# Cache copies on one queue in 4 or 8 parts, value and weight splits on GpSimd, one scale on ScalarE, in a two-layer attention kernel

## The reference, cut to what matters

```python
x = x + einsum('bsi,boi->bso', x, weight[adapter_ids])        # layer 0, 8 batches of 128x512
# layer 1: attention, 32 query heads, 8 key heads, D = 128
q, k, v = x@Wq.T, x@Wk.T, x@Wv.T                               # q: 8 x 4 x 128 columns, k and v: 8 x 128
q = rope(rmsnorm(q, q_norm_w)); k = rope(rmsnorm(k, k_norm_w))
kc, vc = k_cache[block_table], v_cache[block_table]            # 16 pages of 32 rows for each batch
scores = einsum(q, concat(kc, k)) / sqrt(D)                    # 512 cached keys and 128 new ones
probs = softmax(where(valid, scores, -1e30))
x = x + (probs @ concat(vc, v)) @ Wo.T
```

## Time and profile before

| what | value |
|---|---|
| median of 2 runs | 1092.32 us (1089.48 and 1095.16) |
| the profiled execution's own time | 1094.0 us |
| its span in the profile | 1092.0 us |
| PE busy | 977.4 us, 90% of the span |
| DVE busy | 920.3 us, 84% |
| POOL busy | 863.5 us, 79% |
| ACT busy | 796.4 us, 73% |
| mean granted TensorE clock | 0.97 of full speed |
| moved by DMA | 173.69 MB, mean 159 GB/s |

### The profile page before, as it was taken

The page is one execution under the profiler, slowest core; times in us unless marked ns, Lnnn a source line. Parts: engine busy times, 40 slices in busy tenths (PEclk is TensorE's granted clock), DMA queues, the critical chain, the costliest instruction groups (busy, mean ns, idle before and its releaser), DMA issues.

```text
span 1092.0 us, 20813 instructions
## 1 busy us (share of the span) xinstructions
PE 977.4 (90%) x5617; PEld 559.3 (51%) x5617; DVE 920.3 (84%) x1942; ACT 796.4 (73%) x2202; POOL 863.5 (79%) x1184
## 2 busy tenths in 40 slices
PE   6787997789868999989998999899998999899997
PEld 4344554455434555545554555455555555455554
DVE  6576876578868999989997999979997999899994
ACT  4364655468677888878887888878887888777873
POOL 3656567558858998889898998889888988989881
PEclk9889999899999999999999999999999999999999
DMA  8688977738897777766778677876776777757862
GB/s 256 174 230 239 246 229 221 207 106 160 179 187 137 142 154 157 138 136 142 158 140 162 128 144 157 148 145 140 154 139 139 153 158 140 130 99 133 152 140 64
DMA packets 505733, 173.69 MB, mean 159 GB/s; under 512 B 429121, under 2 KB 487762, under 8 KB 505618
## 3 DMA queue, kind: packets, MB, share of 16 engines
q1 hardware_dynamic: 482752, 149.76, 65.5%
q10 hardware_dynamic: 21714, 20.25, 6.1%
q0 software_dynamic: 1152, 2.36, 0.8%
HBM read 98.11 MB, written 31.86 MB: 119 GB/s over the span
## 4 chain that ended last, share of the span: by engine, by line
PE 42%; DVE 19%; issue 4%; POOL 2%; ACT 2%; DVEq 0%; POOLq 0%; ACTq 0%
PE S L1729 10%; DVE pr L1359 5%; DVE pr L1331 5%; DVE sm L1344 4%; PE Y L1655 4%; PE Y L1657 4%; PE Y L1656 4%; PE Q L1656 3%; PE Q L1655 3%; PE Q L1657 3%; PE O L1655 2%; PE O L1656 2%; PE O L1657 2%; PE T L1661 2%; POOL wl L644 2%
## 5 line engine op out<-in xcount | busy, mean ns | idle before, releaser
L1359 DVE SCALAR_TENSOR_TENSOR pr<-pr,rc,upper 128x640 f16<-128x640 f32 x220 | 235.2, 1069 | 20.5 <-ACT upper L1025 13.8
L1331 DVE CUSTOM_DVE_ANT_0 pr<-S,mask,rst 128x640 f32<-128x640 f32 x256 | 224.4, 876 | 30.8 <-PE S L1729 19.2
L1025 ACT ACTIVATE upper<-pr,rc 128x640 f16<-128x640 f32 x220 | 170.3, 820 | 75.7 <-DVE rc L1347 75.6
L1045 ACT ACTIVATE pr<-pr,nb 128x640 f32<-128x640 f32 x256 | 209.6, 819 | 17.5 <-DVE nb L1331 14.5
L1729 PE MATMUL S<-kh,qh 128*128 128x320 f16 x512 | 113.0, 303 | 41.9 <-DVE nb L1331 41.9
L754 POOL TENSOR_TENSOR m<-m 128x512 f32<-128x512 f32 x63 | 81.7, 1297 | 78.1 <-DVE m L1403 78.1
L1729 PE MATMUL S<-kl,qh 128*128 128x320 f16 x512 | 112.3, 301 | 0.9 <-POOL kl L644 0.9
L1729 PE MATMUL S<-kh,ql 128*128 128x320 f16 x512 | 112.5, 302 | 0.0
L644 POOL TENSOR_TENSOR wl<-wraw,wh 128x512 f16<-128x512 f32 x71 | 104.2, 1468 | 5.9
L1729 PEld LDWEIGHTS S<-kh,qh 128*128 128x128 f16 x512 | 45.9, 99 | 116.1 <-DVE nb L1331 71.1
L1655 PE MATMUL Q<-wh,xh 128*128 128x512 f16 x256 | 99.9, 390 | 4.1 <-issue 2.8
(11 more groups left out here) (218 smaller groups left out, 2719.4 us busy)
## 6 DMA issues: line engine op xcount, KB each, us to landing
wraw<-in_wall SPq DMA_DIRECT2D x74, 256.0 KB, 3.5
cache_rows<-in_kv ACTq DMA_DIRECT2D x80, 224.0 KB
rawk<-cache_rows SPq DMA_DIRECT2D x55, 256.0 KB
vraw<-cache_rows SPq DMA_DIRECT2D x55, 256.0 KB, 4.6
cache_rows<-in_kv SPq DMA_DIRECT2D x36, 224.0 KB
second<-in_lw SPq DMA_DIRECT2D x4, 1024.0 KB
first<-in_lw SPq DMA_DIRECT2D x3, 1024.0 KB
cache_rows<-in_kv SPq DMA_DIRECT2D x16, 192.0 KB, 3.6
```

The lines of the kernel that those rows point to most:

```text
L1025: e.activation(upper16[:, g, :], pr[:, slot(u, g), :], ACT.Copy, scale=rc[:, u % 2, g:g + 1]).then_inc(a_f1, 1)
L1045: e.activation(pr[:, slot(u, g), :], pr[:, slot(u, g), :], ACT.Exp, bias=nb[:, u % 2, g:g + 1], scale=-1.0, accum_out=sm[:, u % 2, g:g + 1 ...
L1331: e.tensor_tensor_reduce(pr[:, slot(u, g), :].rearrange("p (a n) -> p a n", a=2), S[:, :, 0:320], mask[:, u % NB, :].rearrange("p (a n) -> ...
L1359: e.scalar_tensor_tensor(out=lower16(u, g), in0=pr[:, slot(u, g), :], scalar=rc[:, u % 2, g:g + 1], in1=upper16[:, g, :], op0=ALU.mult, op ...
```

## The change

Each piece in a sentence:

- NL goes from 9 to 4. Units 4 to 8 load keys and values from the copy.
- All copies are issued by SP, 16 pages (one batch) in each of periods 0 to 7, batches 4, 5, 6, 7, 0, 1, 2, 3. Batches 4 to 7 copy 16 rows a page in 4 parts (pieces of 4 KB), batches 0 to 3 copy 14 rows in 8 parts (2 KB).
- The tables: weight loads, squares and high parts come about one period earlier, the low parts stay about where they were. The two slots in a period are gone. DVE's three low parts of head 0 go to POOL.
- The value split of periods 1 to 8 goes from DVE (2 operations) to POOL (3).
- `score_scales` goes from POOL to ACT, between `q_hi` and `new_k_hi`. `norm` makes the variance in one operation rather than two. `kvr` is made in two operations rather than one (`value_back`).
- The first unit's key split goes to ACT and DVE; chunk 5 of head 0 has its high part on POOL.

```diff
-NL = NB + 1
+NL = 4
-COPY_SP = (0, 1, 1, 1, 1, 1, 1, 2, 0, 1, 1, 1, 2, 0)
-COPY_ACT = (2, 2, 3, 2, 2, 3, 3, 2, 1, 0, 0, 0, 0, 0)
-LO_DVE = {(0, 6): (1, 1), (0, 7): (1, 1), (0, 9): (1, 1)}
+LO_POOL = {(0, 6): 1, (0, 7): 1, (0, 8): 1, (0, 9): 1, (1, 0): -4, (1, 1): -4, (1, 2): -3,
+           (1, 3): -3, (1, 4): -2, (1, 5): -2, 0: -6, 1: -5, 2: -4, 3: -3, 4: -2, 5: -2,
+           6: -1, 7: 0, 8: 1, 9: 1}
+LOAD_AT = {(1, 0): -8, (1, 1): -8, (1, 2): -7, (1, 3): -7, (1, 4): -7, (1, 5): -6,
+           0: -12, 1: -11, 2: -11, 3: -10, 4: -9, 5: -8, 6: -6, 7: -6, 8: -5, 9: -5}
...
+def copies_of(period):
+    return [((period + NL) % NB, t) for t in range(NGRP)] if 0 <= period < NB else []
...
         def copy_page(e, b, k, number):
-            rows = slice(2 if b >= NL - NB else 4, 2 * NK)
-            e.dma_start(copy[rows, b, k, :].rearrange("r (s n) -> s r n", s=16),
-                        kv[rows, bass.ds(number, 1), :].rearrange("r a (s n) -> (a s) r n", s=16)
+            rows, parts = (slice(2, 2 * NK), 8) if b < NL else (slice(0, 2 * NK), 4)
+            e.dma_start(copy[rows, b, k, :].rearrange("r (s n) -> s r n", s=parts),
+                        kv[rows, bass.ds(number, 1), :].rearrange("r a (s n) -> (a s) r n", s=parts)
...
             def load_w(hk, c):
-                if hk >= 1:
+                if hk >= 1 and c < 4:
+                    e.wait_ge(w_lo[0], parts_made(hk - 2, 0) + c + 1)
+                elif hk >= 1:
                     e.wait_ge(w_lo[group(c)], parts_made(hk - 1, group(c)))
...
             for i in range(0, NA):
+                if i + 3 < NB:
+                    load_x(i + 3)
+                if NL <= i + 1:
+                    load_v(i + 1)
                 if 2 <= i + 1 < NB:
                     load_mask(i + 1)
                 next_weights(i)
                 if i + 3 < NL:
-                    for t in range(NT):
+                    for t in range(2, NT):
                         load_kt(e, kt_regs, i + 3, t)
-                        if t == (1 if i else 0) and i + 3 < NB:
-                            load_x(i + 3)
-                else:
-                    load_k(e, i + 3)
                 for b, t in copies_of(i):
                     copy_pages(b, t)
+                if i + 3 >= NL:
+                    load_k(e, i + 3)
...
+            def score_scales(j):
+                e.wait_ge(g_pow, j + 1)
+                e.wait_ge(g_kvr, j + 1)
+                if j >= 2:
+                    e.wait_ge(v_max, 4 * (j - 1))
+                e.activation(rst[:, j % 2, 0:G], pw[:, j % 2, 0:G], ACT.Copy,
+                             scale=f32(kvr[:, j % 2, 1:2])).then_inc(a_rst, 1)
```

More of the change, by code:

```diff
@@ L99, in at_period @@
         for c in range(NWC):
-            own = hk == 0 or (table is LO_POOL and (hk, c) in LO_DVE)
-            if not ((hk, c) in table or (c in table and not own)):
-                continue
-            at = table[(hk, c)] if (hk, c) in table else table[c]
-            if at == (period - NB * hk if slot is None else (period - NB * hk, slot)):
+            general = c in table and hk > 0 and not (hk == 1 and c < 6)
+            at = table.get((hk, c), table[c] if general else None)
+            if at is not None and NB * hk + at == period:
                 found.append((hk, c))
     return found
-def copies_of(period, act=False):
-    if not 0 <= period < len(COPY_SP):
-        return []
-    first = sum(COPY_SP[:period]) + sum(COPY_ACT[:period]) + (COPY_SP[period] if act else 0)
-    return [((k // NGRP + NL) % NB, k % NGRP)
-            for k in range(first, first + (COPY_ACT if act else COPY_SP)[period])]
+def copies_of(period):
+    return [((period + NL) % NB, t) for t in range(NGRP)] if 0 <= period < NB else []
 def build(nc, x, xt, lw, wall, kv, ids_lens, table, pages, qkw, consts, iota, out):
@@ L358, in build @@
         id_reg = nc.sync.alloc_register("id")
-        copy_regs = [nc.scalar.alloc_register(f"copied{j}") for j in range(12)]
+        copy_regs = [nc.scalar.alloc_register(f"copied{j}") for j in range(4)]
         def bc(src, n):
@@ L569, in _ @@
             e.dma_start(kwc[:, :], qkw[D:2 * D].unsqueeze(1)).then_inc(d_kwc, 16)
-            for t in range(2):
+            for t in range(3):
                 load_kt(e, kt_regs, 0, t)
@@ L649, in _, with split_w @@
             w_scaled = [0]
-            def split_w(period, place):
-                for hk, c in at_period(LO_POOL, period, place):
+            def split_w(period):
+                for hk, c in at_period(LO_POOL, period):
                     e.wait_ge(w_hi[group(c)], hi_made(hk, c))
@@ L866, in _ @@
                     gather_v(j, 1)
+                if i == 0:
+                    keys_hi(j)
+                    keys_lo(j)
+                q_sum(j)
+                norm(j)
                 if i:
                     keys_hi(j)
-                norm(j)
-                keys_lo(j)
-                split_w(i, 0)
-                split_w(i, 1)
+                    keys_lo(j)
+                split_w(i)
                 if 1 < j < NL:
@@ L1006, in v_squares, with first_keys_hi @@
                 square(v_left[:, u % 2, :], vraw[:, u % 3, :], kvss[:, u % 2, 0:1]).then_inc(a_kvss, 1)
[L1008 to L1017 removed]
+            def first_keys_hi():
+                e.wait_ge(g_kvs, 1)
+                e.activation(kh[:, 0, 0:512], raw_k(0), ACT.Copy, scale=k_scale(0)
+                             ).then_inc(made_kh, 1)
+            def score_scales(j):
[5 more added lines that the diff above has]
+                             scale=f32(kvr[:, j % 2, 1:2])).then_inc(a_rst, 1)
             def upper_plane(u, g):
@@ L1071, in _ @@
             split_chunk(0, 4)
-            split_chunk(0, 5)
+            w_square(0, 1)
             l0_hi(0)
-            for c in range(1, 4):
+            for c in range(2, 4):
                 w_square(0, c)
-            key_squares(0)
             for c in range(4):
                 split_chunk(0, c)
+            key_squares(0)
             k_squares(0)
@@ L1114, in _ @@
                     exp(i, 1)
+                    for t in range(2):
+                        load_kt(e, copy_regs, 3, t)
                 q_squares(j)
@@ L1512, in _ @@
             k_sum(0)
+            first_keys_lo()
             q_lo(0)
```

271 lines of the change are left out of this document (112 added, 159 removed), and 12 rows, old and new, of tables (HI_ACT, LO_POOL, SQUARES).

## The result

The changed kernel takes 1202.01 us (median of 2 runs, 1201.38 and 1202.63), against 1092.32 before. The ratio is 1.100, with a 95% interval of 1.088 to 1.113: slower, on the predicted side and inside the range, 19 us under the predicted 1221. The profiled execution took 1202.63 us; its span is 1200.8 us, its mean granted TensorE clock 0.923.

The account below looks back on a forecast made before the run. The kernel was taken as bound early by when transfers land, later by PE. 1094.0 + 151 (periods 0 to 8) - 13.7 (periods 9 to 13) - 10.8 (heads' starts) gave 1220.5, forecast 1221 us, range 1075 to 1285.

Parts of the forecast that it names:

- The deciding choice: Copies in periods 0 to 7: one engine per outermost index, so four or eight engines carry them; chance 0.78.
- Rival A: Periods 0 to 8: copies use all 16 engines, a batch takes 11 us, the whole 1066 us; chance 0.13.
- the heads' starts: Six new heads after period 14: POOL late by 0.95 us less, and 0.85 goes in period 25; -10.8 us.
- Rival B: Periods 0 to 8: copies on all 16 engines, but POOL becomes the early bound; 1090 us, chance 0.09.
- The first copy: Period 0: SP issues it at about 52 us, after x, weight chunks and eight 16 KB loads.
- The price of a piece: Copies: 177 ns per 4 KB and 94 ns per 2 KB piece; a batch takes 45.3 or 21.1 us.
- what lies around the copies: Periods 0 to 8: other loads add 7, 7 and 3 us to the first two batches, then 8 + 3.
- The weights that hold SP: Periods 4 and 5: chunk loads waiting for POOL's low parts delay the copies; keys come 15 us late each time.
- Periods 9 to 13: With all copies in by then, their 13.7 us over five plain periods go: -13.7 us.
- Period 25 and its like: Period 25, 0.87 us over a plain one: period 24's second POOL chunk moves to 25, so 0.85 us goes.
- the plain periods: From period 14 on, at 14.3 us each: PE stays full, so 0 change.
- The new wait of ACT's `rst`: Heads' starts: ACT's `rst` waits for POOL's power, ahead of new keys and last exponential; -3 to +10 us, 0 taken.

Follow-up runs that it names:

- e1: The changed kernel with every page's copy cut into 16 parts, nothing else touched; 1096.48 us, ratio 1.0005 to the kernel before.
- e4: The changed kernel with all copies cut in 8 parts, so batches 4 to 7 too; 1127.51 us.
- e3: The kernel before with its copies in 4 parts instead of 16 and one repeated group of pages left out; 1191.1 us.
- e9: e1 with SP's load of the next keys moved ahead of the copies of the same period; 1072.65 us.
- e5: The changed kernel with SP's weight loads of periods 0 to 7 moved behind the period's copies and keys' load; 1188.24 us.
- e12: The changed kernel with POOL's variance in two operations again and nothing else changed; 1186.48 us.
- e6: e1 with `score_scales` moved back from ACT to POOL, behind the keys' low part and ahead of the weight chunks; 1097.79 us.

## Why the prediction was right, and where it was off

**The deciding choice was right.** A copy runs on as many engines as it has parts: e1, e4 and e3 show it, each by its own way. Rival A was wrong in its condition, and e1, which meets the condition, shows its size too: 1096 and not 1066. The 16 engines finish early, but the load of the keys stands behind 16 copies that end inside the period, so the keys wait 54 us in seven periods, where the rival had 18 in two. e9 takes that away and comes to 1073. Its gain at the heads' starts didn't come either. Rival B (POOL as the early bound) needed spread copies; e9 opens period 9 at 239.0 with POOL's value split in place, so it was not the bound there either.

**The first copy** starts at 51.7 (predicted 52).

**The price of a piece and what lies around the copies were too high: these terms were mis-sized.** 177 ns for 4 KB, on four engines, gave 45.3 us for a batch and, with 11 for what lies around it, 56 between one unit's keys and the next. The trace has 49.7 and 50.2 between the keys and 159 ns for a piece; batch 5 takes 40.5 us, so about 9 are left for what lies around. A 2 KB piece was taken at 94 ns and took 89, a batch of them 19.8 us for 21.1. The prices taken were thus a tenth and a twentieth too high. The line was drawn through the means of two queues, over all 16 engines of the busy kernel. Keys of units 4, 5, 6, 7 and 8 were forecast at 159, 215, 271, 306 and 341; they came at 143, 193, 243, 277 and 312. The first is 16 us early: 5 of it are the cheaper pieces (the two batches ran from 53.3 to 98.5 and from 101.1 to 141.6), the other 11 are room that the step left around them (17 us booked, 5.4 used). The next two lose 6 each, the last two under 1.

**The weights that hold SP**: predicted waits of 15 us in periods 5 and 6, measured 15.5 and 15.7, and e5 takes about half of them away. The step has batch 0's copies issued 11 us after unit 6's keys arrive; it was 11.5 (254.52 after 243.05). But periods 7 and 8, for whose keys (issued in periods 6 and 7) 1 to 2 us were forecast, waited 9.4 and 8.5: the copies of two batches in 8 parts still hold the keys there, as in e4 (9.4 and 8.4). So the opening of period 9 is +125.5 us for the forecast +151. The shape makes 108.9 of it (after minus e1); the place of the keys' load another 28.7 (e1 minus e9); all else of the change gains 12 (239.0 against 251.1).

**Periods 9 to 13**: -13.0 measured, -13.7 forecast. ACT's waits there for values from the copy are gone.

**The heads' starts failed as a sum.** -10.8 was forecast for 14 to 63, -0.6 came. The step says that POOL "loses the second variance operation (0.27)" and takes that as gain alone. The operation had kept POOL's key split behind DVE's work on the probabilities; e12 puts 17.2 us on it. A term of the other sign was missing altogether.

The terms that stand there came out only in part, as e12 shows, where the collision is undone and the stage gains 17.8 us against before. The periods just ahead of a new head give 7.8 us for the forecast 5.7; the wait of PE there comes to 2.8 us for the forecast 2.3, and in four of six the clock stays full (one of six before), which the step didn't count. Period 25 and its like give 8.1 for 5.1, but the period behind each takes 8.4 back: POOL's second chunk went there, and is late there. The remaining 10.3 come from the plain periods, which went from 14.3 to 13.8 us, where the step took 0 because "PE stays full". No run tells why. So a gain near the forecast would have been luck in part. The new wait of ACT's `rst` costs nothing that shows (e6), as taken.

**The tail** gained 3.1 us, where 0 was taken.

Sum by these terms: 1094.0 + 125.5 - 13.0 - 0.6 - 3.1 = 1202.8, and the profiled execution took 1202.6. That the forecast is 18 us off and not 26 is luck: it has 25.5 us too much in the first stage and books 10.2 of gain too much in periods 14 to 63. The four and eight engines aren't luck.

## What to carry to other kernels

Before you make pieces larger, look at the outermost index of both sides of a transfer: it decides how many engines work, and 4 and 8 in place of 16 cost this kernel 109 us, although the pieces were two to four times as large; a load issued behind such a transfer waits for it even where it needs nothing of it. A load that a compute engine waits for belongs ahead of the bulk copies of its period (28.7 us by period 9 here, for moving one line). And an operation that looks like pure cost can hold two engines apart: after you take one away, compare the mean of every unchanged group, as a group that has grown points at the collision.
